# Layer 1's sampling: a semaphore for each band of window loads, every other band issued by GpSimd

## What is computed

```python
x_proj = x_nhwc @ w_in + b_in                     # the image that is sampled
x1 = gelu(layernorm(depthwise_conv3x3(x)))
offset = x1 @ w_off + b_off                       # 4 groups x 9 taps x (x, y)
mask = softmax((x1 @ w_mask + b_mask), over the 9 taps)
out = sum over taps of mask * bilinear(x_proj, pixel + tap + offset)
out = out @ w_out + b_out
y = batch_norm(out); return y * sigmoid(y)
```

## Time and profile before

| | us |
|---|---|
| median of 3 runs | 1339.34 |
| lowest, highest | 1337.37, 1342.71 |
| the profiled execution, as timed | 1340.9 |
| its span, first to last instruction | 1339.1 |

### The profile page before, as it was taken

How to read it: one execution, slowest core, us unless ns; L and a number is a source line. 1 busy time by engine, 2 the same in 40 slices (tenths; PEclk the granted TensorE clock), 3 DMA queues, 4 the chain that set the end, 5 groups by cost and what they waited for, 6 DMA issues and landing times. The chain is left out here.

```text
span 1339.1 us, 31514 instructions
## 1 busy us (share of the span) xinstructions
PE 1143.8 (85%) x13280; PEld 610.0 (46%) x13280; DVE 872.9 (65%) x1188; ACT 651.5 (49%) x1108; POOL 643.8 (48%) x465
## 2 busy tenths in 40 slices
PE   3976896969479999999999578899999999999658
PEld 1443485834236666666666342233333333334323
DVE  3787953678856666667664678556767676666623
ACT  1657134645547677767765270244444444455310
POOL 2000000022257767767775030388888888888400
PEclk9985597979669999999999785799999999998869
DMA  4100212212155554555552032000000000010003
GB/s 93 24 1 26 52 56 70 59 26 54 35 162 159 167 156 158 169 163 153 163 161 63 1 65 77 1 1 2 1 1 1 2 1 2 1 67 16 0 19 72
DMA packets 59804, 83.80 MB, mean 63 GB/s; under 512 B 21911, under 2 KB 44056, under 8 KB 58888
## 3 DMA queue, kind: packets, MB, share of 16 engines
q1 hardware_dynamic: 59496, 81.43, 21.0%
q10 hardware_dynamic: 160, 0.30, 0.1%
HBM read 66.62 MB, written 12.10 MB: 59 GB/s over the span
## 5 line engine op out<-in xcount | busy, mean ns | idle before, releaser
L2263 POOL TENSOR_TENSOR arena_sb<-arena_sb 128x768 f32<-128x768 f32 x168 | 323.7, 1927 | 122.1 <-ACT arena_sb L2224 101.8
L2224 ACT ACTIVATE arena_sb<-ps 128x768 f32<-128x768 f32 x216 | 174.8, 810 | 245.3 <-PE ps L2153 243.1
L2278 DVE TENSOR_REDUCE arena_sb<-ps 128x4 f32<-128x1536 f32 x108 | 189.0, 1758 | 127.7 <-PE ps L2120 125.9
L2153 PE MATMUL ps<-arena_sb 33*64 33x384 f32 x1728 | 188.1, 504 | 11.4 <-ACT arena_sb L2224 5.4
L2165 PE MATMUL ps<-arena_sb 64*64 64x384 f32 x1728 | 169.2, 490 | 3.4 <-ACT arena_sb L2231 3.4
L1632 PE MATMUL ps<-arena_sb 120*64 120x216 f32 x1536 | 165.4, 355 | 0.6 <-DVE arena_sb L1756 0.6
L1782 POOL TENSOR_SCALAR xp_sb<-xp_sb 128x384 f32<-128x384 f32 x69 | 103.0, 1493 | 92.8 <-ACT xp_sb L1681 90.9
L2120 PE MATMUL ps<-arena_sb 32*128 32x384 f32 x864 | 114.9, 607 | 11.2 <-DVE arena_sb L2278 5.2
L1751 DVE TENSOR_TENSOR arena_sb<-ps,arena_sb 120x384 f32<-120x384 f32 x216 | 119.9, 555 | 2.5 <-ACT arena_sb L1688 2.5
L1632 PEld LDWEIGHTS ps<-arena_sb 120*64 120x64 f32 x1536 | 101.8, 137 | 41.7 <-ACT xp_sb L1681 14.9
L1698 ACT ACTIVATE xp_sb<-ps 128x432 f32<-128x432 f32 x192 | 102.4, 533 | 28.0 <-PE ps L1632 28.0
(11 more groups left out here) (248 smaller groups left out, 1646.3 us busy)
## 6 DMA issues: line engine op xcount, KB each, us to landing
xn_sb<-far_hats SPq DMA_DIRECT2D x96, 270.0 KB
arena_sb<-far_hats SPq DMA_DIRECT2D x48, 270.0 KB
arena_sb<-pixel_major SPq DMA_DIRECT2D x96, 120.0 KB, 3.9
xp_sb<-projected SPq DMA_DIRECT2D x72, 60.0 KB
far_hats<-xp_sb SPq DMA_DIRECT2D x24, 162.0 KB
pixel_major<-arena_sb SPq DMA_DIRECT2D x24, 108.0 KB
projected<-arena_sb SPq DMA_DIRECT2D x12, 208.0 KB
x_sb<-in_x SPq DMA_DIRECT2D x4, 576.0 KB, 8.1
```

The lines of the kernel that those rows point to most:

```text
L2153: mm = pe.matmul(p_scores(g)[64 * i:64 * i + 64, h, :], kp[own, key:key + 64], qp[own, PIX * b2 + CH * ib:PIX * b2 + CH * ib + CH], start= ...
L2224: act.activation(pt[g % SLOTS].rearrange("p (h n) -> p h n", h=2), p_scores(g), ACT.Exp)\
L2263: pool.tensor_tensor(acc, first, pt[g % SLOTS], ALU.add).then_inc(S["pool_added"], 1)
L2278: v.tensor_reduce(part.rearrange("p (a u j) -> p a u j", a=3, u=NB)[:, a, :, jc], p_m(m), AX.X, ALU.max)\
```

## The change

The one semaphore for windows becomes eight, one for each band. PE waits at the head of each band's sums for that band's six windows of the batch, where it waited for all 48 once per batch. SP issues bands 0, 2, 4 and 6, POOL bands 1, 3, 5 and 7, each with the same wait for the sums of batch 0 ahead of batch 1, and each waits at its end for its own bands. Sizes, places and contents of the transfers are the same.

```diff
-         ("turned", "at", "spread", "b_act", "b_dve", "xw", "sums", "half", "mixed", "y", "gated", "gate", "added", "moments")}
+         ("turned", "at", "spread", "b_act", "b_dve", "sums", "half", "mixed", "y", "gated", "gate", "added", "moments")}
+    XW = [signal(k, f"ws_xw{ty}") for ty in range(NTY)]
...
-    LOADS = NTX0 * NTY * 16
+    LOADS = NTX0 * 16
...
+    def windows_of(eng, b, ty):
+
+        rows = k["proj"][PQ * (PQ * b + TH * ty):PQ * (PQ * b + TH * ty + VH), :].rearrange("(y x) c -> y x c", x=PQ)
+        for t in range(NTX0):
+            eng.dma_start(xw(ty, t, slice(0, 2)).rearrange("p h c -> p (h c)"), rows[:, TW * t:TW * t + VW, :])\
+                .then_inc(XW[ty], 16)
...
                 if ty == 0:
                     pe.wait_ge(S["b_act"], SLOTS * (b + 1))
                     pe.wait_ge(S["b_dve"], SLOTS * (b + 1))
-                    pe.wait_ge(S["xw"], LOADS * (b + 1))
+                pe.wait_ge(XW[ty], LOADS * (b + 1))
...
         @block.sync
         def _(sp):
             for b in range(2):
-                for ty in range(NTY):
+                for ty in range(0, NTY, 2):
                     if b:
                         sp.wait_ge(S["sums"], ty + 1)
-                    rows = k["proj"][PQ * (PQ * b + TH * ty):PQ * (PQ * b + TH * ty + VH), :].rearrange("(y x) c -> y x c", x=PQ)
-                    for t in range(NTX0):
-                        sp.dma_start(xw(ty, t, slice(0, 2)).rearrange("p h c -> p (h c)"), rows[:, TW * t:TW * t + VW, :])\
-                            .then_inc(S["xw"], 16)
-            sp.wait_ge(S["xw"], 2 * LOADS)
+                    windows_of(sp, b, ty)
+            for ty in range(0, NTY, 2):
+                sp.wait_ge(XW[ty], 2 * LOADS)
+
+        @block.gpsimd
+        def _(pool):
+            for b in range(2):
+                for ty in range(1, NTY, 2):
+                    if b:
+                        pool.wait_ge(S["sums"], ty + 1)
+                    windows_of(pool, b, ty)
+            for ty in range(1, NTY, 2):
+                pool.wait_ge(XW[ty], 2 * LOADS)
```

## The result

The changed kernel took 1,326.46 us (median of 4 runs, 1,325.60 to 1,327.44), the kernel before 1,340.65 beside it: a ratio of 0.989, 95% interval 0.9868 to 0.9911. Run again it was 1,324.70 (median of 6 runs) against 1,339.65, ratio 0.9886 (0.9864 to 0.9907). So it is faster by 14 to 15 us, 1.1%. Forecast: 1,325.6.

What follows compares the result with a forecast made beforehand. TensorE's sums were held by one wait for all 48 transfers, paced by SP's queue. 11.59 + 2.41 - 0.3 = 13.7 us off the 1,339.34 median gave 1,325.6 us, range 1,321 to 1,331.5.

Steps and rivals of the forecast that it cites:

- First term: Batch 0, start of the sums: they begin at 204.71 instead of 216.30, 11.59 us less.
- Second term: Batch 0, first to third sums: 4.69 us at full clock instead of 7.10, so 2.41 us less.
- rival 3: TensorE's clock drops in the new pause anyway: the 2.41 us go, 11.3 stay, 1,328.0 us; chance 0.15.
- The 14 waits: TensorE's added waits from the split semaphore: 0 to 1.4 us, taken as 0.3 us.
- Sum for the block: First-layer sampling block: 11.59 + 2.41 - 0.3 = 13.7 us less.
- POOL's price: Time per transfer issued on POOL's queue: estimated 1.0 us, bounds 0.80 and 3.2, in time up to 1.68.
- The claim that the semaphores alone close the hole: With SP issuing all bands, band 7 lands at 216.3, needed at 222.8; batch 1 lands at 245.8, needed from 246.7.
- Rival 1: Odd bands' sums in batch 1 wait for POOL's issues, costing from 1.68 us each; 1,350 at 2.2; slower 0.08.
- Rival 2: POOL stands still during VectorE's 24 copies, late from 1.20 us per issue; 1,335 us at 1.4; chance 0.03.
- Rival 4: Two queues share DMA engines that can't deliver faster, bands come at the old pace; 1,339 us; chance 0.01.
- The forecast's 1.6 "after its issue": Landing time of a window's transfer: 1.6 us after its issue, taken from SP's own wait at the block's end.

Runs made afterwards that it cites:

- changed again: The changed kernel itself run once more, with nothing altered; 1,324.70 us, ratio to before 0.9886.
- split only: Against the changed kernel, SP issues all 48 windows of each batch and POOL none, still a semaphore per band; 1,325.65 us, ratio to before 0.9896.
- queues only: Against the changed kernel, TensorE waits once per batch for all 48 windows, with SP and POOL both still issuing; 1,325.31 us, ratio to before 0.989.
- POOL issues all: Against the changed kernel, POOL issues all 48 windows of each batch and SP none; 1,328.89 us (one run).
- VectorE copies: The changed kernel plus 12 unused SBUF-to-SBUF copies on VectorE from the block's start, beside POOL's first issues; 1,330.89 us (one run).
- POOL's windows in 4 DMAs: Against the changed kernel, each of POOL's windows goes as 4 DMAs of 32 channels instead of one of 128; 1,355.12 us, ratio to before 1.011.
- 4 fillers: The changed kernel plus 4 unused matmuls on TensorE ahead of each batch's first sums; 1,325.17 us, ratio to before 0.9882.
- 14 fillers: 14 unused matmuls ahead of each batch's first sums, added to the changed kernel (1,327.76 us, ratio 0.991) and to split only (1,328.38 us, 0.9915).

## Why the prediction was right, step by step

- **First term, 11.59 us: right.** The sums begin 1.12 us behind the spread's last matmul, as in batch 1, instead of 12.71 (idle times): 11.59 measured. It is the value for a late spread, as in the one profile that the prediction had. With an early spread the first sums come 26.8 us behind SP's first issue instead of 40.07, a gain of 13.2, which the prediction did not see.
- **Second term, 2.41 us: too large.** Measured 7.10 - 6.04 = 1.06 in the first profile and 1.55, 1.83 and 1.05 in the next three kernels without that wait (changed again, split only, queues only); where POOL issues all it was nothing (7.37). The step that failed is "if the clock stays up over the 1.1 us": it did not in the first profile, which is rival 3, though rival 3 took away all 2.41 and the drop cost 1.35, as it lasts 3 us here and 5 before. Over all profiles with an open pause, the clock fell in batch 0 in the four with a late spread and stayed up in the three with an early one; in batch 1, from which the forecast had argued, it stayed up in eight of ten and fell in two (split only, VectorE copies). And where it did stay up in batch 0, a stop of 0.37 to 0.65 us that the forecast did not know took its place.
- **The 14 waits, 0.3 us: nothing**, by the rounds of 2.68 and 1.81 us.
- **Sum for the block, 13.7.** Profiles show 13.0 for the first pair, a late spread on both sides. There the error in the second term is partly made up elsewhere: the batch 1 spread took 14.23 us where it took 14.67 before. Over three profiles of before (mean 105.0) and two of after (91.4) it is 13.6. That this lies so close to 13.7 is luck: the second profile of after had an early spread, which gives 1.6 us that no term of the sum holds and stands in for what the second term lacks. The medians differ by 14.2 and 15.0, up to 1.4 us more than the block. An early spread in some of the executions that were timed would account for part of it; how many had one isn't known. Stages behind the block differ by as much between profiles of one and the same kernel (the spans of before run from 1,339.1 to 1,342.0), so this rest is not put down to the change.
- **POOL's price, 1.0 us: wrong, on the safe side.** It is 0.57 from issue to issue, below even the lower bound of 0.80. That bound rested on the thought that POOL can't be quicker than SP at the same transfer. The upper end, 3.2 us from the ratio of 4.2 in arithmetic, was no guide to issuing either. It did no harm, since nothing depended on it up to 1.68.
- **The claim that the semaphores alone close the hole: right, with a slip in its working.** The text let SP's batch 1 start at 205.9 and end at 244.2. But SP, which issues all 48 in that version, is busy with batch 0 until 215. Batch 1 then ends at 254.4. It was in time only because the waits go by band; with one wait for all 48 at 245.3 the sums would have been some 10 us late, by an estimate from 254.4 and the 1.5 to landing. (That kernel is not the kernel before, whose sums started 11.6 us later and hid just this.)
- **Rival 1** was tried by raising the price to 2.28 us a window: 1,355.1 measured where its formula gives 1,353.8. **Rival 2** is real for copies from SBUF to SBUF and absent for those of this stage. The prediction's "all 24 copies would stop POOL" was too wide: they read PSUM, and the rule names copies from SBUF to SBUF. **Rival 4** is excluded: with both queues at work, from 178 to 192 us, the DMA share was 0.67 and the rate 181 GB/s, against 0.28 and 81 GB/s before.

## What to carry over

A wait for all of a stage's transfers costs what the last of them takes, though the first consumer needs one eighth of them: count per consumer what must have landed when, before adding queues. Of two remedies for one wait, try each alone: here each gave all of it, and the one without a second queue has 2.6 us of cover in batch 1 while the one with it has 28 (POOL's last issue begun at 228.7 and landed 2.3 later, its sums at 259.8). A wait also hides the scatter of what runs beside it: here 1.6 us of turns counted only once it was gone. And a gain counted from a clock that stays up needs a range of its own: of 2.41 us on paper, between nothing and 1.83 came.

## What was not expected of the hardware

- POOL issues a transfer of 120 rows every 0.57 us, whether the rows hold 512 or 128 bytes, against 0.80 on SP. Its recorded durations grow in a long row of issues (579 to 826 ns over 48, up to 1,562 over 192 small ones) while the pace stays; they overlap, so pace must be read from starts.
- Landing is not later on POOL's queue, as far as the rows go: median 2.5 us from the start of the issue. SP's own wait at the end of the block, 2.1 us in the changed kernel and 1.6 before, counts from the end of its last issue; with that issue's 0.75 it is 2.9 and 2.4. The forecast's 1.6 "after its issue" is of the second kind.
- A VectorE copy from SBUF to SBUF holds a POOL issue back until it is done (0.88 us beside copies of 0.835).
- TensorE stops for 0.37 to 0.65 us with nothing to wait for that the profile shows, and always at the same place of its list: in the second sums, behind 45 of their 48 records (changed again, split only, POOL's windows in 4 DMAs), and behind 37 with 4 fillers, whose 8 records stand ahead. So it goes with the place in the list and not with the time since the first sums. Kernels that came to this place at half clock or behind 14 fillers show no stop. While it stops, in the changed kernel's second profile, the DMA engines are 27% busy. The trace counts one transfer of 16 KB on a queue of the kind "instruction" in the 3 us ahead of the stop (list of DMA queues of that profile, 203.6 to 206.4 us):

```profile
q8 instruction: 1, 0.02, 2.5%
```

It runs from 203.66 to 204.78, and TensorE goes on at 206.35, 1.6 us behind its end. In the other three stops that time is 1.2, 1.6 and 1.5 us. The nine profiles without a stop come to the same place 2.3 us or more behind the end of the transfer that stands at this point of their traces. That fits a late supply of instructions. It is read from times alone; no experiment moved the transfer, so the cause stays argued and not shown.
